# A graph network's first layer: where GpSimd waits for gathered rows

## What is computed

```python
h = relu(layernorm(x))                                   # 12500 x 64
# first layer
z = concat([h[src], edge_attr_32]) @ W1 + b1             # 400000 x 64
m = silu(silu(layernorm(z) * g1 + be1) @ W2 + b2)
agg = segment_sum(m, dst)
x = x + layernorm(silu(concat([agg, h]) @ Wu + bu)) * gn + bn
# second layer
h = relu(layernorm(x))
agg = segment_sum(h[src], dst)
x = x + relu((h + agg) @ M1 + c1) @ M2 + c2
```

## Time and profile before

| | us |
|---|---|
| median of 3 runs | 6198.23 (6190.43 to 6201.92) |
| span of the profiled execution | 6194.4 |
| first layer's gathers, first to last | 196.8 to 4467.2, 4270.4 |
| GpSimd busy in that stretch | 3070.34 |
| the rest of the span behind it | 1727.2 |

### The profile page before, as it was taken

The page is one execution under the profiler, slowest core; times in us unless marked ns, Lnnn a source line. Parts: engine busy times, 40 slices in busy tenths (PEclk is TensorE's granted clock), DMA queues, the critical chain, the costliest instruction groups (busy, mean ns, idle before and its releaser), DMA issues. The chain is left out here.

```text
span 6194.4 us, 75337 instructions
## 1 busy us (share of the span) xinstructions
PE 3949.3 (64%) x23603; PEld 3229.6 (52%) x23603; DVE 2502.4 (40%) x5222; ACT 2070.8 (33%) x2908; POOL 4331.5 (70%) x4165
## 2 busy tenths in 40 slices
PE   6455555555555555555555555555576999999999
PEld 5234344444444444444444434444455888888886
DVE  6322222222232222222222222222376777777751
ACT  2022222222222222222222222222235777777751
POOL 3777777777777777777777777777656777777861
PEclk9566767677676667776766676676658999999995
DMA  3111111111111111111111111111121000000011
GB/s 93 44 36 35 37 36 36 37 36 37 37 36 36 36 37 37 36 36 37 36 37 37 36 36 36 37 37 36 27 51 25 22 22 22 22 22 22 22 25 33
DMA packets 256727, 216.83 MB, mean 35 GB/s; under 512 B 138460, under 2 KB 188953, under 8 KB 256007
## 3 DMA queue, kind: packets, MB, share of 16 engines
q0 software_dynamic: 133248, 136.74, 10.2%
q1 hardware_dynamic: 123271, 77.59, 4.3%
HBM read 199.53 MB, written 14.40 MB: 35 GB/s over the span
## 5 line engine op out<-in xcount | busy, mean ns | idle before, releaser
L719 POOL DMA_INDIRECT gat<-layer_rows,idx x3992 | 4115.7, 1031 | 1477.5 <-issue 1057.8
L764 PE MATMUL ps<-one_hots,edge_buffers 128*128 128x80 f32 x3128 | 687.5, 392 | 1890.9 <-DVE cT L808 1890.9
L764 PEld LDWEIGHTS ps<-one_hots,edge_buffers 128*128 128x128 f32 x3128 | 621.3, 295 | 2243.3 <-issue 2243.3
L1015 DVE TENSOR_TENSOR edge_buffers<-ps,gat 128x512 f32<-128x512 f32 x391 | 270.2, 691 | 2948.1 <-DMA gat<-layer_rows,idx 2390.0
L1574 ACT ACTIVATE node_buffers<-ps 125x800 bf16<-125x800 f32 x1152 | 954.2, 839 | 342.3 <-PE ps L1625 278.8
L970 ACT ACTIVATE edge_buffers<-ps,gcol 128x512 f32<-128x512 f32 x391 | 302.6, 774 | 2142.9 <-PE ps L739 2142.8
L732 PE MATMUL ps<-w1e,edge_buffers 128*128 128x256 f32 x1564 | 739.6, 625 | 114.7 <-DVE edge_buffers L1015 110.7
L1604 PE MATMUL ps<-edge_buffers,node_buffers 125*128 125x192 bf16 x7200 | 764.8, 247 | 0.0
L1604 PEld LDWEIGHTS ps<-edge_buffers,node_buffers 125*128 125x128 bf16 x7200 | 666.4, 140 | 12.3 <-issue 12.2
L1625 PE MATMUL ps<-node_buffers 128*128 128x200 bf16 x4608 | 607.3, 255 | 59.8 <-ACT node_buffers L1574 45.6
L1683 DVE TENSOR_TENSOR node_buffers<-ioh,node_buffers 128x1600 bf16<-128x1600 bf16 x576 | 567.3, 985 | 0.0
(11 more groups left out here) (182 smaller groups left out, 3075.4 us busy)
## 6 DMA issues: line engine op xcount, KB each, us to landing
gat<-layer_rows,idx POOLq DMA_INDIRECT x3992
edge_buffers<-in_edge_quads SPq DMA_DIRECT2D x391, 128.0 KB, 2.1
node_buffers<-in_x SPq DMA_DIRECT2D x5, 625.0 KB
layer_rows<-node_buffers SPq DMA_DIRECT2D x25, 125.0 KB
residual_rows<-node_buffers SPq DMA_DIRECT2D x5, 625.0 KB
layer_rows<-node_buffers SPq DMA_DIRECT2D x5, 625.0 KB
node_buffers<-residual_rows POOLq DMA_DIRECT2D x25, 125.0 KB, 4.4
out<-node_buffers SPq DMA_DIRECT2D x25, 125.0 KB
```

What stands on the lines that cost most here:

```text
L719: pool.indirect_dma_start(out=gat[:, j, c, :], out_offset=None, in_=table[:, :], in_offset=bass.IndirectOffsetOnAxis(ap=idx[:, half, j, c: ...
L764: mm = pe.matmul(to[:, 0:2 * WIN], rows_of[:, 2 * k:2 * k + 2, :].rearrange("p c f -> p (c f)"), oh[:, j, 2 * k:2 * k + 2, :].rearrange("p ...
```

## The change

In the first layer's loop the wait behind the gathers of every third block goes. In its place every block from the third on waits, ahead of its gathers and together with the waits that already stand there, until the rows of the last block but one have landed (`lagged(e, j, 2)` gives the slot of block n - 2).

```diff
--- before.py
+++ after.py
@@ -894,11 +894,12 @@
                             wait(pool, g_idx, rows_before(e, j) + 1)
 
                         wait(pool, g_z, n - AHEAD + 1)
+                        before_last = lagged(e, j, 2)[0]
+                        if n > 1:
+
+                            wait(pool, g_gat[before_last], rows_before(e, j - 2) * (16 * BC) + 16 * BC)
                         wait_alone(pool, "gpsimd")
                         gather(pool, ptab, j // UN, s, g_gat[s])
-                        if n % 3 == 2 and n + 1 < BLOCKS:
-
-                            wait(pool, g_gat[s], rows_before(e, j) * (16 * BC) + 16 * BC)
                 with pool.If(flagged(pool) == 0):
                     rounds(step, 0)
```

## The result

| | before | after |
|---|---|---|
| median, us | 6200.07 (6190.43 to 6205.46, 4 runs) | 5929.67 (5927.38 to 5931.6, 4 runs) |
| ratio | | 0.9563 (95% interval 0.955 to 0.9577) |
| span of the profiled execution | 6194.4 | 5925.7 |
| first layer's gathers, first start to last end | 4270.4 | 3997.5 |
| behind them, to the end | 1727.2 | 1731.5 |

The change makes the kernel 270.4 us faster, and all of it comes from the first layer. The forecast was 250 us less, 5948 us; the measured time lies 18 us under it, and 6 us under the low end of the range (5936).

The account below looks back on a forecast made before the run. GpSimd's gathers in the first layer were taken as the bound. Pauses -247, new wait 0 and stretching -3 gave -250: span 6194.4 to 5944.4, with 3.8 for the median 5948 us; range 5936 to 5990.

Parts of the forecast that it names:

- What bounds the kernel: First layer: GpSimd's gathers set the rate; 3910 us of gathers, 247 of pauses, 114 of stretching, together 4271.
- Part 1: First layer: the wait behind every third block goes, 1.90 us over the normal step, 130 times: -247 us.
- Part 2: First layer: the new wait for the last block but one stops GpSimd's queue, never the engine: 0 us.
- Part 3: First layer: gathers lengthened beside certain VectorE instructions, 114 us before; change taken as -3 us, ends -9 and +58.
- Part 4: First layer: z is done with three blocks, some 30 us, in hand before block n + 4's gathers.
- rival 2: First layer: the pauses kept GpSimd out of VectorE's way; 151 us come back, 6102 us; chance 0.03.
- Rival 3: First layer: the new wait stops the engine too, at every block; +496, 6694 us; chance 0.03.
- rival 4: First layer: transfers or descriptors pile up without the pause; the 247 us return, about 6198 us; chance 0.04.
- Rival 5: First layer: compute becomes the bound at 10.27 us a block; costing half the gain, 6074 us; chance 0.02.

Follow-up runs that it names:

- the first pair: Kernel before and changed kernel, unchanged, in the first measurement, each profiled: 6200.07 and 5929.67 us, ratio 0.9563.
- the second chip: Both kernels run again unchanged and profiled on another chip: before 6188.67 us, ratio 1.0002; changed 5918.22 us, 0.9566.
- the quick chip: Chip of the follow-ups where the kernel before takes 6188.67 us and the changed one 5918.22, ratio 0.9566; the first measurement's chip is of this kind.
- the late ones: Three chips where the kernel before takes 6760, 6780 and 6879 us; the changed kernel on one: 6805.33 against 6779.66, ratio 1.0035.

## Why the prediction was right, and where it was wrong

**What bounds the kernel.** Right on the chip it was made for: the layer is GpSimd's stream of gathers, and both traces after it are the prediction's sum with one term gone.

**Part 1, the pause.** Right, by undoing it: 1.90 us x 130 in the first trace, 1.97 x 130 in the second; removed, the borders show the bare 0.305 us.

**Part 2, the new wait.** Right, and the reason is shown rather than argued: leaving the wait out changes nothing (5919.0 and 5918.22), and moving it one block nearer costs 764 us. The queue passes it 9.1 us ahead of the block's first gather, as the earlier trace rows let one work out.

**Part 3, the stretching: this is the step that failed, by its size.** I took -3 us, from ends of -9 and +58. It measured -26 in the first pair and -17.5 in the second. Two things were off. The prediction read the ordinary blocks' stretching as a constant of the kernel, 0.27 us. It depends on where in the gathers' cycle VectorE starts: with 0.06 us more of landing it was 0.22 us, 13 us less over the 261 blocks that never followed a pause, and 13 us more went with the other 130 (0.33 to 0.23). And having worked out -9 from the earlier trace rows it took -3, drawn towards a mean (0.29) that contained the very blocks that would go. The blocks behind a pause themselves were read from one, 0.44, where the mean is 0.33; the earlier trace rows had no more of them. With -26 in place of -3 and the 4.3 us by which the rest grew, the sum gives 5929.3, against 5929.67 measured. With -17.5 it would be 5938, just inside the range; the 9 us that go with the landing, which was that execution's and not the change's, took the time below 5936. On the second chip the gain is as large, 269 us, for another reason: its pauses cost 256 us. The low end was too high for the same reason: nothing in the rows bounded the landing's effect at -9, since a phase can move either way.

**Part 4, who is late next.** Right on the quick chip, where GpSimd waits for nothing (L795 once aside), and wrong on three others. z has three blocks, some 30 us, in hand in these traces, but a single chip's trace can't tell how much TensorE will be late on another.

**The rivals.** The pauses gave no shelter (rival 2): the stretching fell. Rival 3's mechanism and price are real, 764 us where 743 was worked out, but one block of distance away. Its margin was put at about 9 us of later landing; by the prediction's own rows it is 7.6 (from 2010.76 to the start of the next block's last gather, 2009.60 + 7 x 1.25). The pause isn't needed for the transfers (rival 4): the median gather is 0.944 to 0.947 us without it. Rival 5, another bound, fell on the quick chip and is what happens on the late ones; there it took not half but all of the gain and 0.35% more.

## What to carry to other kernels

Where an engine's own queue runs ahead, ask of a wait how far back its event lies, not how often it stands there: the same wait is free one block further back and costs 1.9 us a time at the nearest block. Read an idle entry by its length, since its name only tells the last event before it. And treat small interference between two engines as a phase, with bounds on both sides: putting one VectorE instruction elsewhere in its list, at the same work, gave 50 us more. Before trusting the names of waits, see whether the trace has all of its events.

## What the runs showed of the hardware that I had not expected

- One program takes 6187 to 6200 us on two chips and 6760 to 6879 on three, and its runs on one chip lie within 0.7% of each other. On the late ones ScalarE starts up to 37.8 us after the recorded end of the matmuls that it needs, while VectorE's, ScalarE's and GpSimd's instructions keep their lengths. With 12.4 us a block in place of 11.6 to 11.8 the lateness is gone from this layer, on two of the same chips. The cause is open.
- A gather on GpSimd is held by a VectorE instruction with two SBUF inputs that runs as it starts, until 0.125 us before that one's end: in the four traces of the two pairs the medians of measured and worked-out excess agree within 0.005 us, and of 5205 such gathers in all traces 5199 agree to 0.015. One that starts later, or within the 0.03 us before the gather, doesn't touch it (but for the exception above), and isn't lengthened by the gather.
- z, of the same size as the normalisation but with one input in PSUM, stretches nothing: the 219 gathers that start under it in the changed kernel have a median of 0.947 us, as all. The sum of squares, with one input in SBUF and three times as long, stretches none of 103 either.
